# GpSimd instead of ScalarE issues the stores of the x-added results in the last pass of a three-layer graph convolution

## The reference

```python
h = jnp.maximum(_layernorm(x, axis=-1), 0.0)
h = relu(adj @ (h @ W1) + b1)
h = relu(adj @ (h @ W2) + b2)
return x + adj @ (h @ W3) + b3
```

## Time and profile before

| | |
|---|---|
| median of 3 runs (lowest, highest) | 1578.43 us (1577.51, 1580.37) |
| profiled execution's own time | 1577.23 us |
| its span, first to last instruction | 1575.4 us |
| granted clock of TensorE | 1.00 over the whole span |
| PE busy | 1569.8 us, 7638 instructions |
| DVE busy | 878.7 us |
| ACT busy | 643.5 us |
| POOL busy | 530.6 us |
| pass3 in the trace | about 1326 us to the end |

### The profile page before, as it was taken

One profiled execution on the slowest core, in us unless ns is written; L12 is line 12 of the kernel. 1 busy time (PEld: TensorE's weight loads), 2 busy tenths in 40 slices (PEclk: granted clock), 3 DMA queues, 4 the chain that ended last, 5 costly groups with the idle time before them and its releaser, 6 DMA issues.

```text
span 1575.4 us, 21103 instructions
## 1 busy us (share of the span) xinstructions
PE 1569.8 (100%) x7638; PEld 1352.6 (86%) x7638; DVE 878.7 (56%) x1360; ACT 643.5 (41%) x1145; POOL 530.6 (34%) x488
## 2 busy tenths in 40 slices
PE   9999999999999999999999999999999999999999
PEld 7888889988889898989898989888898888888898
DVE  8983433255453546353545444764665537676766
ACT  5542222233343424233333333543455436555554
POOL 5864554436655545000000003573202333021302
PEclk9999999999999999999999999999999999999999
DMA  6966657555687888454657567783544357898887
GB/s 242 347 192 225 221 181 223 177 161 157 194 273 239 296 265 292 144 178 116 204 150 220 171 209 237 256 274 111 182 130 124 95 167 239 255 326 263 264 271 223
DMA packets 211091, 334.52 MB, mean 212 GB/s; under 512 B 25608, under 2 KB 96896, under 8 KB 210988
## 3 DMA queue, kind: packets, MB, share of 16 engines
q1 hardware_dynamic: 171484, 239.78, 49.6%
q0 software_dynamic: 15680, 55.31, 10.7%
q10 hardware_dynamic: 23824, 38.10, 6.8%
HBM read 243.75 MB, written 89.36 MB: 211 GB/s over the span
## 4 chain that ended last, share of the span: by engine, by line
PE 98%; DVE 1%; DMA 1%; ACT 0%; issue 0%; DVEq 0%; ACTq 0%
PE ps L1820 32%; PE ps L1822 31%; PE ps L1821 31%; PE ps L1910 2%; PE ps L1909 2%; DMA raw<-HX 0%; PE ps L1858 0%; DVE ring L1451 0%; DMA xin<-x 0%; DVE slots L1433 0%; ACT slots L1164 0%; DVE stats L1363 0%; DVE parts L1580 0%; DVE still L1399 0%; DVE parts L1576 0%
## 5 line engine op out<-in xcount | busy, mean ns | idle before, releaser
L1451 DVE TENSOR_TENSOR ring<-raw,ring 128x512 fp32r<-128x512 f32 (+1 forms) x522 | 381.4, 745 | 398.0 <-ACT ring L1202 395.8
L1202 ACT CAST ring<-raw 128x512 fp32r<-128x512 f32 (+1 forms) x564 | 320.2, 576 | 487.4 <-PE ps L1822 392.6
L1820 PE MATMUL ps<-slots,still 128*128 128x512 f32 (+1 forms) x504 | 183.2, 364 | 0.7 <-DVE slots L1433 0.5
L1821 PE MATMUL ps<-slots,still 128*128 128x512 f32 (+1 forms) x504 | 183.1, 363 | 0.0
L1822 PE MATMUL ps<-slots,still 128*128 128x512 f32 (+1 forms) x504 | 183.1, 363 | 0.0
L1820 PE MATMUL ps<-ring,even 128*128 128x512 f32 (+1 forms) x480 | 174.3, 363 | 0.0
L1821 PE MATMUL ps<-ring,even 128*128 128x512 f32 (+1 forms) x480 | 174.3, 363 | 0.0
L1822 PE MATMUL ps<-ring,even 128*128 128x512 f32 (+1 forms) x480 | 174.3, 363 | 0.0
L1820 PE MATMUL ps<-ring,S 128*128 128x512 f32 (+1 forms) x420 | 153.4, 365 | 0.3 <-DVE ring L1451 0.2
L1821 PE MATMUL ps<-ring,S 128*128 128x512 f32 (+1 forms) x420 | 152.8, 364 | 0.0
L1822 PE MATMUL ps<-ring,S 128*128 128x512 f32 (+1 forms) x420 | 152.8, 364 | 0.0
(11 more groups left out here) (160 smaller groups left out, 3022.1 us busy)
## 6 DMA issues: line engine op xcount, KB each, us to landing
raw<-TS SPq DMA_DIRECT2D x160, 256.0 KB, 3.3
raw<-adjT SPq DMA_DIRECT2D x122, 256.0 KB, 3.8
raw<-adjT SPq DMA_DIRECT2D x41, 512.0 KB, 5.0
TS<-made SPq DMA_DIRECT2D x20, 1024.0 KB, 6.7
raw<-TS SPq DMA_DIRECT2D x80, 165.0 KB, 2.8
raw<-HS SPq DMA_DIRECT2D x50, 256.0 KB, 3.2
raw<-P SPq DMA_DIRECT2D x44, 256.0 KB, 4.0
HS<-pair_buf POOLq DMA_DIRECT2D x20, 512.0 KB, 4.7
```

Of the source, the lines that this page charges most:

```text
L1202: act.copy(hi, src).then_inc(hi_done, 1)
L1451: dve.tensor_tensor(lo, src, hi.bitcast(F32), ALU.subtract).then_inc(lo_done, 1)
L1820: pe.matmul(out, st_hi, mv_hi, start=start, stop=False)
L1821: pe.matmul(out, st_hi, mv_lo, start=False, stop=False)
```

## The change

The four stores of each chunk that follow POOL's sums (parts 1 and 4) are issued by POOL, right behind its second sum, where before ACT issued them. They count semaphores of their own (`added_stored`). DVE waits for these before it overwrites e(4) to e(7) in the second and third chunk, and SP waits for them at the end. ACT keeps the stores of parts 5 and 6.

```diff
-            p.steps.append(("finish", (g.chunk, where, half, side, g.free_drained)))
-        if finals:
+            p.steps.append(("finish", (g.chunk, where, half, side, g.free_drained, last, p.final)))
+        if part > 4:
...
-            p.later({1: 4, 4: 20}.get(part, 2), store)
+            p.later(2, store)
...  (SP, at the end)
+            for i in range(4):
+                sp.wait_ge(added_stored[i], 16 * CHUNKS)
...  (ACT, ahead of the stores)
-                    if g.part in (1, 4):
-                        act.wait_ge(finished, plan.final_of[g.chunk, g.part])
-                    else:
-                        act.wait_ge(drained, number)
+                    act.wait_ge(drained, number)
...  (DVE, in the drain)
+                        if g.phase == "pass3" and part in (1, 4) and g.chunk > 0:
+                            dve.wait_ge(added_stored[(0 if part == 1 else 2) + m], 16 * g.chunk)
...  (POOL, behind the two sums of a pair)
+                if last not in (1, 4):
+                    continue
+                for m in range(2):
+                    k = 2 * side + m
+                    pool.wait_ge(finished, final - 1 + m)
+                    pool.dma_start(outT[k * P:(k + 1) * P, columns(half, c)], e(where + m, c)) \
+                        .then_inc(added_stored[where + m - 4], 16)
```

More of the change, by code:

```diff
@@ L821, in gcn_kernel @@
         finished = sem("finished")
+        added_stored = [sem(f"added_stored{i}") for i in range(4)]
         block = ctx.enter_context(nc.Block())
@@ L1798, in _ @@
                     continue
-                c, where, half, side, number = a
+                c, where, half, side, number, last, final = a
                 for m in range(2):
```

## The result

| | before | after |
|---|---|---|
| median of 14 runs | 1579.32 us | 1581.96 us |
| lowest to highest | 1576.92 to 1581.72 | 1579.84 to 1583.48 |
| ratio after/before, 95% interval | | 1.0017, [1.001, 1.0025] |
| profiled execution, own time | 1577.23 us | 1579.84 us |
| its span | 1575.4 us | 1577.7 us |

The changed kernel is slower by 2.6 us, and a ratio of 1 lies outside the interval. With more runs of the kernel before, its median is 1579.32 instead of the 1578.43 that was known ahead. The time is outside the range of 1576.6 to 1580.7; the difference of 0.17% is within the 0.2% that was called no change.

What follows compares the result with a forecast made beforehand. PE was taken to set the time up to its last matmul, with a tail behind. 1577.23 + 0 + 0 + 0 + 0.2 = 1577.4 us, or 1578.6 on the scale of medians; range 1576.6 to 1580.7.

Steps and rivals of the forecast that it cites:

- The tail: Behind PE's last matmul: POOL's last pair lands before the very last store; +0.2 us, bounds 0 and +0.8.
- SP's four waits: At the program's end: four more waits for SP at 0.05 us each, +0.2 us.
- Own time against span: Around the span: the sum started from the profiled execution's own time, 1577.23 us, and added no term for this.
- Inside pass3: Removed waits, POOL's added issues and DVE's added waits during pass3 were each priced at 0.
- the cover: Ring of five places in front of PE: a lead of 4.1 us, over the longest hold of 3.24 us.
- The removed holds at 0: ACT's waits for POOL's sums, 4.6 us in all over three chunks, cost PE nothing; removing them gains 0.
- The rival in which they cost PE: ACT's holds did cost PE, hidden by modelled ends; 4.6 us come back, 1574.0 us; 3%.
- POOL's issues: Behind six second sums: two issues of 554 ns each, 1.1 us a pair, delaying loads of x; cost 0.
- DVE's waits for the stores: Eight waits before e(4) to e(7) are overwritten, 0.05 us each, with some 80 us of room; cost 0.
- The burst: Around 1395, next chunk and third: stores and loads of x delay ring tiles; 4.3 us, 1582.9; 4%.
- The stretched subtractions: DVE beside POOL's sums: two or three subtractions stretched 1.1 us each; +1 us, 1579.6; 6% within the forecast's case.

Runs made afterwards that it cites:

- g2: Kernel before, with only part 4's three pairs of stores moved to POOL, part 1's staying with ACT; 1580.87 us, ratio 1.0014 [1.0005, 1.0023].
- g3: Changed kernel, with ACT still waiting for POOL's sums at the six old places though it stores nothing there; 1582.13 us, ratio 1.0017 [1.0008, 1.0026].
- e3: Kernel before, with two dummy sums on unneeded tiles behind POOL's last work; 1582.03 us, ratio 1.0014 [1.0005, 1.0023].
- e4: Kernel before, with eight dummy sums on unneeded tiles behind POOL's last work; 1586.56 us, ratio 1.0046 [1.0033, 1.0058].
- h3: Kernel before, with five pairs stored three more times each to scratch memory by POOL, 30 stores more; 1593.00 us, ratio 1.0081 [1.0068, 1.0095].
- g1: Kernel before, with ACT's part 1 stores eight tiles behind the drain instead of four, so ACT is not held; 1578.85 us, ratio 1.0001 [0.9992, 1.001].
- h2: Kernel before, with eleven tiny POOL writes behind each of five pairs, delaying its loads of x; 1580.58 us, ratio 1.0003 [0.9994, 1.0012].
- h1: Kernel e1 (last pair stored by ACT), with POOL's loads of x issued ahead of its stores; 1582.17 us, ratio 1.0011 [1.0001, 1.0021].
- e1: Changed kernel, with only the third chunk's part 4 pair stored by ACT again; 1581.31 us, ratio 1.0012 [1.0003, 1.0021].
- f2: Changed kernel, with its stores counted on semaphores that were there before instead of four new ones; 1581.64 us, ratio 1.0016 [1.0007, 1.0025].
- f4: Changed kernel, with already existing semaphores and POOL loading x one pair ahead; 1583.32 us, ratio 1.003 [1.0018, 1.0042].
- f1: Kernel before, with four more semaphores that nothing uses; 1579.44 us, ratio 1.0002 [0.9993, 1.0011].
- e2: Kernel before, with only the third chunk's part 4 pair stored by POOL behind its last sums; 1578.97 us, ratio 1.0 [0.9992, 1.0009].
- f3: Kernel before, with POOL loading x for a pair before it adds the pair ahead; 1581.87 us, ratio 1.0018 [1.0009, 1.0027].
- g4: Kernel before, with only part 1's three pairs of stores moved to POOL; 1579.85 us, ratio 1.0005 [0.9996, 1.0014].
- h4: Kernel g1, with five pairs stored three more times each by ACT, 30 stores more; 1591.11 us, ratio 1.0078 [1.0065, 1.009].

## Why the prediction was wrong, step by step

**The tail is the step that failed.** It was put at +0.2 us with bounds of 0 and +0.8. I counted the issue and the landing, and both held: the pair landed by 1571.6 (I had said 1573.3), before the last store. What I took for "some 0.5 us of waits and closing instructions" held a second path: POOL's last work, then 8.2 us of its closing DRAIN. It was 0.1 us from deciding in the trace of before, and two issues of 0.558 us behind POOL's last sum put it in front. SP's four waits cost nothing: its DRAIN begins 2.1 us behind ACT's last issue before and after. The late end measures +1.4 us in the changed kernel's trace, 1.3 in g2 and 1.5 in g3, and e3 and e4 show the mechanism by dose. In the other kernels with the old end (h3 with its short DRAIN aside) POOL is between 0.5 us early (g1, h2) and 0.3 us late (h1), so the 0.1 us is one execution's figure. Being out 4 us ahead of the very last store was no room, as I had taken it to be: POOL's second issue, where its DRAIN begins, was 6.9 us ahead of SP's DRAIN (1569.2 and 1576.1), and 8.3 were needed.

The tail alone does not make the miss. The sum was 1578.6, and the measured median is 3.4 us above it: 0.9 us by the median of the kernel before, which more runs put higher, 1.2 by the tail, 0.36 outside of the span, and some 0.9 in pass3.

**Own time against span.** The sum took what lies around the span as unchanged. It is 2.18 instead of 1.82 us in all six kernels that move pairs of both parts (after, e1, f2, f4, g3, h1) and in none of the others. Not the semaphores (f1, f2), not the number of POOL's stores (h3) and not the last pair (e1, e2) do it. The +0.36 us is measured; its cause stays open.

**Inside pass3** I had 0 for everything. By means, e1 is 1.7 us slower with the old tail, less 0.36 outside; so about 1.3 us stays, good to 1.4 us. f2, and f4 against f3, point the same way. g2 and g4 don't tell whose pairs it goes with: less their tails they are 0.7 and 0.3 us slower, both within the noise. The traces put it in the third chunk. There the cover that I had worked out does not hold: 4.1 us is the lead for tiles of 512 columns. With 330 columns the casts follow each other every 0.90 us, a cast takes 0.47 us and a subtraction 0.50, so by the same working the lead is 4 x 0.90 - 0.47 - 0.50 = 2.6 us, an estimate. One late tile of `HX` is seen to reach PE there, in four of the traces. Whether that is the whole of it stays open.

**The removed holds at 0** were right, by g1 and g3. The rival in which they cost PE (1574.0) is refuted by g1: with the holds gone and nothing else changed the ratio is 1.0001 [0.9992, 1.001]. Part of the hold was hidden twice, since the tile from `TS` lands late enough to stop ACT for 1.6 us anyway.

**POOL's issues** took 545 to 565 ns against the 554 that I used, and the loads of x 1.6 us later met no new wait at the sums. DVE's waits for the stores appear in no list of waits. The Trainium skill, in "SBUF — State Buffer", the box on DVE blocking DMA, says that GpSimd cannot write the descriptors of a transfer while DVE runs an instruction in a two-port mode. None of the twelve issues was held up, in a stretch where DVE is busy 70 of 100 us; but no row tells the mode of DVE's instructions, so no run here tests that rule.

**The burst** (1582.9) came near in time, but not at the places that I named. Behind part 4 the window from 1400 has 90 matmuls as before. Something like it, a tile that lands late beside POOL's stores and loads, stands in the traces behind part 1 of the third chunk, where I had moved only the loads, by 1.1 us, and priced that at 0; it is worth 0.8 to 1.6 us of PE there and not 4.3. The mechanism is also there with far more traffic, in h3 and h4: with 30 more stores the ring's tiles land about 1 us later, and gaps open in PE's stream. That the total is alike from either queue agrees with the Trainium skill, "DMA: Bandwidth & Descriptors", the section "Issuing engines are not separate DMA queues", which says that all of them run interleaved on the same 16 engines.

**The stretched subtractions** (1579.6) cost nothing at the place that I named. A subtraction beside POOL's first sum took 1.02 us, not 1.8:

```profile
1334.29 1.02 DVE L1451 TENSOR_TENSOR ring<-raw,ring 128x512 fp32r<-128x512 f32 x1 [0.67 <-ACT ring L1205]
```

The mechanism is there in f3. The drain's four sums take 2.5 us of DVE (1372.92 to 1375.43), and behind them seven subtractions at 1.67 us, where PE needs one every 1.36 us, lose another 7 x (1.67 - 1.36) = 2.2 us. Together that is 4.7 us, over the lead of 4.1 us that I had worked out, and PE waits 1.26 us. The Trainium skill, "SBUF — State Buffer", section "Who interferes with whom", says that a DVE instruction with two SBUF inputs contends with a GpSimd one that reads SBUF, and the trace agrees.

No version ran faster than the kernel before by more than its interval; e2 and g1 are equal to it within theirs.

## What to carry to other kernels

Follow the end of a kernel for every engine, not only for the one with the last store: take each engine's last work, add its closing DRAIN, and compare. Here POOL's last instruction has to begin about 8.2 us before the end, so an issue behind its last sum is not free. Work out the cover anew where the tiles get smaller. An engine's idle time under another's name is worth nothing until a kernel without it has run (g1), and moves of 0.1% need such one-edit kernels beside them, because a single trace differs by as much from its start-up alone.

## What the runs showed that was not expected

- The closing DRAIN of POOL takes 7.8 to 8.9 us in most of these kernels, and 3.9, 5.4 and 5.9 us in f2, f4 and h3; DVE's takes 0.74 and ACT's 0.15 in every one. What sets the length of POOL's is open.
- Own time minus span has two values here, 1.80 to 1.87 and 2.17 to 2.18 us as means, and the runs of a kernel keep to one of them.
- The last pair, 165 KB a store, lands in 2.2 and 2.3 us from POOL and took 1.8 and 2.0 us from ACT before; the very last store takes 1.8 us in both kernels.
- A store more costs 0.4 us in pass3 (12.7 / 30 from POOL, 11.8 / 30 from ACT): with its busy PE the pass has little room for more transfers.
- PE's stream in pass3 is the same from kernel to kernel up to the third chunk, in ten of the 18 traces to 0.1 us. What differs from run to run comes ahead of pass3, whose first drain lies between 1329.2 and 1333.1 in the 18 traces, and behind 1533.
